# Attention turns put in another order on every engine, and a slot loop written out, in a fused cross-attention and mixture-of-experts kernel

## What is computed

```python
x = x + _L0_xattn_ref(_layernorm(x, axis=-1), ctx_2048, ...)
x = x + _L0_ffn_ref(_layernorm(x, axis=-1), L0_ffn_gate_w, L0_ffn_w1, L0_ffn_w2)
# attention
q = rms_norm(linear(x, q_w, q_b), norm_q_w)
k_img = rms_norm(linear(ctx_img, k_img_w, k_img_b), norm_k_img_w)
v_img = linear(ctx_img, v_img_w, v_img_b)
img_x = attention(q, k_img, v_img)
return linear(out, o_w, o_b)
# experts
topw, sel = jax.lax.top_k(softmax(x @ gate_w.T), 2)
act = jax.nn.silu(g) * u          # g, u = split(x @ w1.T)
out = sum over the two experts of (act @ w2.T) * topw
```

## Time and profile before

| | us |
|---|---|
| median of 3 runs | 558.54 |
| all runs | 558.28, 558.54, 558.55 |
| the profiled execution | 557.55 |
| its span, first to last instruction | 556.0 |

### The profile page before, as it was taken

How to read it: one execution, slowest core, us unless ns; L and a number is a source line. 1 busy time by engine, 2 the same in 40 slices (tenths; PEclk the granted TensorE clock), 3 DMA queues, 4 the chain that set the end, 5 groups by cost and what they waited for, 6 DMA issues and landing times.

```text
span 556.0 us, 15244 instructions
## 1 busy us (share of the span) xinstructions
PE 444.1 (80%) x4192; PEld 397.1 (71%) x4193; DVE 389.4 (70%) x1215; ACT 315.1 (57%) x934; POOL 301.8 (54%) x531
## 2 busy tenths in 40 slices
PE   1779889898989898989898860599999999999100
PEld 1658778777877787778777650499989999999100
DVE  7448888988988898889888855254545454545284
ACT  5357577767776777677767620255555555555100
POOL 6534357777777777777776646044434443444200
PEclk9779899999999999999999985599999999999655
DMA  7131442222322232213221115423434343331499
GB/s 228 53 109 42 128 125 85 75 80 63 89 70 82 62 91 71 82 60 92 65 80 61 50 40 134 134 88 114 127 109 120 102 124 106 116 110 66 164 399 343
DMA packets 49542, 60.30 MB, mean 108 GB/s; under 512 B 7615, under 2 KB 43082, under 8 KB 49482
## 3 DMA queue, kind: packets, MB, share of 16 engines
q1 hardware_dynamic: 38026, 38.00, 23.5%
q0 software_dynamic: 6528, 16.86, 8.8%
q10 hardware_dynamic: 4928, 4.72, 2.5%
HBM read 32.86 MB, written 23.27 MB: 101 GB/s over the span
## 4 chain that ended last, share of the span: by engine, by line
PE 55%; DVE 11%; issue 9%; ACT 9%; POOL 6%; DMA 5%; SPq 3%; POOLq 0%; ACTq 0%; DVEq 0%
PE bank L1109 13%; PE bank L1110 12%; PE bank L1111 12%; PE bank L1320 4%; DMA we_l<-expert_out 3%; DVE late L835 3%; POOL r_qk L415 2%; PE bank L1117 2%; PE bank L1142 2%; PE bank L1219 2%; PE bank L1339 1%; PE bank L1338 1%; ACT square L599 1%; ACT late L554 1%; SPq L382 1%
## 5 line engine op out<-in xcount | busy, mean ns | idle before, releaser
L527 POOL DMA_INDIRECT expert_out<-probs,late x72 | 69.9, 971 | 100.7 <-ACT probs L720 99.6
L457 POOL DMA_INDIRECT sorted_rows<-row,place_i x64 | 66.0, 1031 | 36.3 <-POOL row L451 25.4
L1067 DVE TENSOR_TENSOR xt_l<-bank,xt_h 128x256 fp32r<-128x256 f32 x72 | 30.6, 425 | 54.9 <-ACT xt_h L702 54.8
L564 ACT CAST qp_h<-bank 32x256 f16<-32x256 f32 x128 | 46.4, 363 | 35.7 <-PE bank L1142 33.4
L841 DVE TENSOR_TENSOR qp_l<-bank,qp_h 32x256 f16<-32x256 f32 x128 | 53.3, 416 | 6.0 <-ACT qp_h L564 2.9
L1109 PE MATMUL bank<-we_h,xt_h 128*128 x144 | 53.4, 371 | 0.1
L1074 DVE SCALAR_TENSOR_TENSOR probs<-xn,late,bank 128x176 f32<-128x176 f32 x72 | 28.6, 398 | 33.1 <-ACT xn L708 33.1
L1109 PE MATMUL bank<-we_h,at_h 128*128 x144 | 46.5, 323 | 1.1 <-issue 0.6
L1110 PE MATMUL bank<-we_l,xt_h 128*128 x144 | 47.1, 327 | 0.0
L1111 PE MATMUL bank<-we_h,xt_l 128*128 x144 | 47.0, 326 | 0.0
L708 ACT ACTIVATE xn<-bank 128x176 f32<-128x176 f32 x72 | 22.9, 317 | 38.8 <-PE bank L1111 38.8
(11 more groups left out here) (194 smaller groups left out, 1571.2 us busy)
## 6 DMA issues: line engine op xcount, KB each, us to landing
late<-sorted_rows SPq DMA_DIRECT2D x72, 129.0 KB, 2.1
we_f<-w_exp SPq DMA_DIRECT2D x32, 152.0 KB, 2.5
v_bd<-v_sb SPq DMA_DIRECT2D x128, 34.0 KB, 1.9
ctx_in<-ctx_t SPq DMA_DIRECT2D x32, 128.0 KB, 2.4
we_h<-expert_out SPq DMA_DIRECT2D x8, 512.0 KB, 6.9
we_l<-expert_out SPq DMA_DIRECT2D x8, 512.0 KB, 15.5
x<-x SPq DMA_DIRECT2D x3, 1024.0 KB, 6.0
out<-we_h ACTq DMA_DIRECT2D x8, 256.0 KB, 13.3
```

Source lines behind the costliest of these rows:

```text
L457: pool.indirect_dma_start(sorted_rows, bass.IndirectOffsetOnAxis(ap=place_i[:, t.slot // 2, k, t.par:t.par + 1], axis=0), row[:, k, t.slot ...
L527: pool.indirect_dma_start(expert_out, bass.IndirectOffsetOnAxis(ap=hs[:, r, D:D + 1].bitcast(U32), axis=0), y_sb[:, r % YRING, :], None, b ...
L564: act.copy(q_part(qp_h, t, g), q_bank(g)).then_inc(S["q_h_ready"], 1)
```

## The change

All four computing engines get a new order within each attention turn. `inv_sqrt` on GpSimd is parted: the addition of epsilon is `add_eps`, so that `ln1` becomes `ln1_root` and `ln1_shift`, and `ln2` becomes `ln2_veps` and `ln2_root`, one turn later. `send` loses its first instruction, which becomes `set_ids`. VectorE's `ln2_mean` moves one turn on. `ctx_hi`, `ctx_lo` and the load of the context go one tile further ahead, and `xt_hi`, `k_hi`, `tr_x` and `tr_k` go from the head of a turn to the end of the turn before. The slot loops of all five engines are written out. No computation is added or taken away.

```diff
@@ -341,8 +341,8 @@
         sp.dma_start(sorted_rows[NE * REG:ROWS, :], pad_rows[:, :]).then_inc(pads_sent, 16)
 
         def turn(j, s):
-            if Tile(j, s + 2).live:
-                load_ctx(Tile(j, s + 2))
+            if Tile(j, s + 3).live:
+                load_ctx(Tile(j, s + 3))
             if Tile(j, s + 1).live and (not isinstance(j, int) or j * SKEW + s + 1 >= 2):
                 load_weights(Tile(j, s + 1))
             if Tile(j, s).live:
@@ -407,17 +408,22 @@
             pool.tensor_tensor(we_l[:, cols], we_f[:, t.par, :], we_h[:, cols].bitcast(F32),
                                ALU.subtract).then_inc(S["we_ready"], 1)
 
-        def inv_sqrt(t, out_, tmp, in_, scale, eps, ready, mid, done_):
+        def add_eps(t, out_, in_, scale, eps, ready, done_):
 
             need_alone(pool, pool_passed, ready, t.n + 1)
-            pool.tensor_scalar(tmp, in_, scale, eps, ALU.mult, ALU.add).then_inc(mid, 1)
-            need_alone(pool, pool_passed, mid, t.n + 1)
-            pool.tensor_tensor(out_, tmp, half_neg[:, 0:tmp.shape[1]], ALU.pow).then_inc(done_, 1)
-
-        def ln1(t):
+            pool.tensor_scalar(out_, in_, scale, eps, ALU.mult, ALU.add).then_inc(done_, 1)
+
+        def inv_sqrt(t, out_, in_, ready, done_):
+
+            need_alone(pool, pool_passed, ready, t.n + 1)
+            pool.tensor_tensor(out_, in_, half_neg[:, 0:in_.shape[1]], ALU.pow).then_inc(done_, 1)
+
+        def ln1_root(t):
             need_alone(pool, pool_passed, S["xn_ready"], t.n - 1)
-            inv_sqrt(t, rstd[:, t.slot, :], veps[:, t.slot, :], mean_var[:, t.par, 1:2], 1.0, 1e-5,
-                     S["ln1_mean"], S["ln1_veps"], S["ln1_rstd"])
+            add_eps(t, veps[:, t.slot, :], mean_var[:, t.par, 1:2], 1.0, 1e-5, S["ln1_mean"], S["ln1_veps"])
+            inv_sqrt(t, rstd[:, t.slot, :], veps[:, t.slot, :], S["ln1_veps"], S["ln1_rstd"])
+
+        def ln1_shift(t):
             need_alone(pool, pool_passed, S["ln1_rstd"], t.n + 1)
             pool.tensor_scalar(shift[:, t.par, :], mean_var[:, t.par, 0:1], rstd[:, t.slot, :], -1.0, ALU.mult, ALU.mult
                                ).then_inc(S["ln1_shift"], 1)
...
@@ -460,20 +471,26 @@
                 ).then_inc(row_sent[t.slot], 16)
 
         def turn(j, s):
-            if Tile(j, s + 1).live:
-                ctx_lo(Tile(j, s + 1))
             if Tile(j, s + 2).live:
-                ln1(Tile(j, s + 2))
+                ln1_root(Tile(j, s + 2))
+            if Tile(j, s - 4).live:
+                ln2_root(Tile(j, s - 4))
             if Tile(j, s).live:
                 qk_rms(Tile(j, s))
-            if s % 2 == 0 and Tile(j, s - 6).live:
-                weights(Tile(j, s - 6), Tile(j, s - 5), (s - 6) // 2 % 2)
+            if Tile(j, s - 5).live:
+                set_ids(Tile(j, s - 5))
+            if Tile(j, s).live:
+                weights_lo(Tile(j, s))
             if Tile(j, s - 6).live:
                 send(Tile(j, s - 6))
+            if Tile(j, s + 2).live:
+                ctx_lo(Tile(j, s + 2))
+            if s % 2 == 1 and Tile(j, s - 5).live:
+                weights(Tile(j, s - 5), Tile(j, s - 4), (s - 5) // 2 % 2)
+            if Tile(j, s + 2).live:
+                ln1_shift(Tile(j, s + 2))
             if Tile(j, s - 3).live:
-                ln2(Tile(j, s - 3))
-            if Tile(j, s).live:
-                weights_lo(Tile(j, s))
+                ln2_veps(Tile(j, s - 3))
 
         setup(pool.memset(ident[:, :], 0.0))
         setup(pool.memset(half_neg[:, :], -0.5))
@@ -493,8 +510,9 @@
                                  base=0, pattern=[[-1, P]], channel_multiplier=1))
         setup(pool.affine_select(out=upto[:, :, :], in_=upto[:, :, :], compare_op=ALU.is_ge, fill=0.0,
                                  base=0, pattern=[[1, NE], [-1, NE]], channel_multiplier=0))
-        ln1(Tile(0, 0))
-        ln1(Tile(0, 1))
+        for n in range(2):
+            ln1_root(Tile(0, n))
+            ln1_shift(Tile(0, n))
         ctx_lo(Tile(0, 0))
         for base in (0, -NH):
             after()
@@ -519,6 +537,7 @@
         for q in (qp_h, qp_l):
             pool.memset(q[:, :, :, :, :, :].rearrange("p u b c g l -> p (u b c g l)").bitcast(F32), 0.0
                         ).then_inc(q_cleared, 1)
+        ctx_lo(Tile(0, 1))
         turns_sp(pool, turn)
 
 
@@ -643,14 +662,6 @@
                 t.quads_ok = not static or t.n >= 4
                 t.at = t.n if static else bass.ds(t.n, 1)
                 return t
-            if tile(0).live:
-                xt_hi(tile(0))
-            if tile(1).live:
-                k_hi(tile(1))
-            if tile(-1).live:
-                ln1_norm(tile(-1))
-            if tile(-1).live:
-                ctx_hi(tile(-1))
             if tile(1).live:
                 t = tile(1)
                 t.first = isinstance(j, int) and t.n == 0
@@ -660,18 +671,26 @@
             if tile(0).live:
                 k_square(tile(0))
             if tile(0).live:
+                v_copy(tile(0))
+            if tile(0).live:
                 q_square(tile(0))
             if tile(3).live:
                 att_hi(tile(3))
+            if tile(-1).live:
+                ln1_norm(tile(-1))
+            if tile(-2).live:
+                ctx_hi(tile(-2))
             if tile(0).live:
-                v_copy(tile(0))
-            if tile(0).live:
+                k_scale(tile(0))
                 weights_hi(tile(0))
-                k_scale(tile(0))
+            if tile(2).live:
+                softmax_exp(tile(2))
             if tile(4).live:
                 row_copy(tile(4))
-            if tile(2).live:
-                softmax_exp(tile(2))
+            if tile(0).live:
+                k_hi(tile(0))
+            if tile(-1).live:
+                xt_hi(tile(-1))
             if s % 2 == 1 and tile(5).live:
                 gap_exp(tile(5), tile(4), (s - 5) // 2 % 2)
 
@@ -691,6 +710,8 @@
         act.wait_ge(pool_setup, SETUP_POOL_FIRST)
         act.activation(bias_f, bias_f, ACT.Copy, scale=zero_one[:, 1:2]).then_inc(bias_parts_ready, 1)
         ln1_norm(t)
+        xt_hi(t)
+        ctx_hi(Tile(0, 1))
         split_hi(1)
         turns_sp(act, turn)
         send_pads(act, 1)
...
@@ -957,41 +980,43 @@
                 t.at = t.n if static else bass.ds(t.n, 1)
                 t.sent = t.quad * 32 if t.quads_ok else None
                 return t
-            ahead = tile(-2) if tile(-2).live else None
+            n = j * SKEW + s if isinstance(j, int) else None
+            if tile(1).live:
+                k_lo(tile(1))
             if tile(0).live:
                 xt_lo(tile(0))
-            if isinstance(j, int) and j == s == 0:
+            if n == 0:
                 rest_of_setup()
-            if tile(1).live:
-                k_lo(tile(1))
+                ln1_stats(tile(-2), x_second)
             if tile(2).live:
                 find_max(tile(2))
-            if ahead:
-                n = j * SKEW + s + 2 if isinstance(j, int) else None
-                ln1_stats(ahead, {2: x_second, 8: x_third, 9: x_rest}.get(n))
+            if tile(4).live:
+                ln2_mean(tile(4))
             if tile(2).live:
                 neg_max_hi(tile(2))
+                neg_max_lo(tile(2))
             if tile(3).live:
                 invert_sums(tile(3))
-            if tile(2).live:
-                neg_max_lo(tile(2))
+            if tile(-2).live:
+                ln1_mean(tile(-2))
             if tile(3).live:
                 normalise(tile(3))
-            if ahead:
-                ln1_mean(ahead)
             if tile(1).live:
                 q_lo(tile(1))
+            if tile(3).live:
+                att_lo(tile(3))
             if tile(4).live:
                 ln2_norm(tile(4))
-            if tile(3).live:
-                att_lo(tile(3))
+            if tile(-3).live:
+                ln1_stats(tile(-3), {5: x_third, 13: x_rest}.get(n))
+            if n == 0:
+                fold_gate()
+            if tile(0).live:
+                q_scale(tile(0))
             if s % 2 == 1 and tile(5).live:
                 route(tile(5), tile(4), (s - 5) // 2 % 2)
-            if isinstance(j, int) and j == s == 0:
-                fold_gate()
             if tile(0).live:
                 gate_of_x(tile(0))
-                q_scale(tile(0))
             if tile(3).live:
                 residual(tile(3))
             if s % 2 == 0 and tile(4).live:
@@ -1275,29 +1300,32 @@
 
                 return min(value, NT) if static else value
 
-            if tile(0).live:
-                tr_x(tile(0))
-            if tile(1).live:
-                tr_k(tile(1))
+            if tile(3).live:
+                weigh(tile(3))
             if tile(2).live:
                 t = tile(2)
                 t.first = static and i == 2
                 score_max(t)
-            if tile(3).live:
-                weigh(tile(3))
             if tile(1).live:
                 tr_q(tile(1))
```

(31 more changed lines are left out.)

20 lines of the change are left out of this document (12 added, 8 removed).

## The result

The kernel after took 561.1 us (median of 20 runs, 557.06 to 563.2), the kernel before 558.17 in the same set (20 runs): a ratio of 1.0044, with a 95% interval of 1.0024 to 1.0064. The forecast was 539.0, the range 532.5 to 547. The prediction was wrong: instead of 3.5% faster, the kernel came out 0.4% slower.

A forecast was written before the change was run, and what follows sets the result against it. Attention was taken as bound by GpSimd in heavy turns, by GpSimd and TensorE in light ones. Gains of 12.8 us there and 6.7 in the experts, 19.5 together, took 557.55 to 538.05, median 539.0 us; range 532.5 to 547.

The forecast's parts named there:

- the part on TensorE: Attention stage: TensorE's pieces summed to 8.2 us, `tr_q` finding its keys split; with the late exponential a turn becomes 8.35.
- D: Rival at the sends: behind `weights_lo` GpSimd empties, then prepares, 0.82 atop 0.30; pair 19.5, time 565 us; chance 0.04.
- GpSimd's sum: Attention stage: GpSimd's turn as one loop from `r_qk` to `r_qk`, 9.53 us heavy and 8.34 light.
- the 0.30 chosen: GpSimd: the first send was taken to start 0.30 us after `weights_lo`, its preparing hidden behind that instruction.
- B: Rival at the sends: their preparing isn't hidden, 0.5 more each turn, pair 18.9, time about 553 us; chance 0.10.
- the 0.82: GpSimd's wait in us ahead of the first send in the profile, read as preparing the transfer, ended by no other engine.
- The heavy turn: GpSimd's attention turn with `weights` in it, put at 9.53 us and bound by GpSimd.
- The light turn: GpSimd's attention turn without `weights`, put at 8.34 us, bound by GpSimd and TensorE both; the wait for `q_square` gone.
- TensorE's turn of 8.35: Attention stage: pieces of 8.2 us plus 0.15 for the late exponential; the light half of the 17.88 pair.
- The forecast for the experts: Expert stage: writing out the slots removes the cost of four loop edges and the entry, 6.7 us, the upper bound.
- The 16 pairs of the sum: Attention stage: 16 pairs of turns, each 17.88 instead of 18.70 us, gain 12.8 us; filling and draining left as they are.
- one slow stretch more or less: Clock rival: a stretch of TensorE at half the clock, 6.8 us long, moves the time by up to 2.7 us.

The follow-up runs named there:

- e20: The kernel after, unchanged, run again on another chip: 532.81 us, ratio 0.960.
- e0: The kernel before, unchanged, profiled once more: 556.33 us, a single run.
- e7: The kernel after with GpSimd's two sends moved ahead of `weights_lo`: 565.02 us, ratio 1.012.
- e10: The kernel before with one change, `weigh` ahead of `score_max` on TensorE: 567.4 us, ratio 1.014.
- e13: The kernel after with `score_max` ahead of `weigh` again and GpSimd's sends ahead of `weights_lo`: 564.31 us, ratio 1.012.
- e14: The kernel after with `score_max` ahead of `weigh`; sends ahead of `weights_lo` in turns with `weights`, behind it in turns with `choose`: 535.73 us, ratio 0.960.
- e17: The kernel after, unchanged, run again on another chip beside e18: 561.01 us, ratio 1.005.
- e19: The kernel after, unchanged, run again on one more chip: 559.43 us, ratio 1.001.
- e1: The kernel after with `score_max` put back ahead of `weigh` on TensorE: 545.86 us, ratio 0.977.
- e11: The kernel after with one wait more: `score_max` waits until TensorE's own products of `weigh` are reported: 578.79 us, ratio 1.035.
- e6b: The kernel after with GpSimd's two sends moved behind `ctx_lo`, 0.7 us later: 570.92 us, ratio 1.022.
- e9b: The kernel after with each indirect send replaced by a plain transfer of the same bytes, rows in token order: 537.53 us, ratio 0.964.
- e16: As e14, GpSimd's order by turn, but with `weigh` ahead of `score_max` as in the kernel after: 530.44 us, ratio 0.954.
- e18: e16 unchanged, run again on the same chip as e17: 544.42 us, ratio 0.975.

## Why the prediction was wrong

- **The step that failed** is in the part on TensorE: its pieces were taken at their modelled length and their readers as starting when they end, "so that `tr_q` finds its keys split". That the order of `weigh` and `score_max` could matter was not weighed, and none of the rivals had it. In the execution measured, reports were held until 0.6 us behind the second send, so those of `score_max` and `tr_q` came at 3.1 us, and the long turn became 10.53 instead of 9.34 (e20), the short one 8.97 instead of 8.36. From the seventh `tr_q` to the last are 243.3 us, where 12.5 pairs at 17.88 make 223.5: **19.8** of the 22.1 us that were missed. The experts' part missed 0.8 in this pair of traces. The other 1.5 are a balance that I did not split: the turns up to the seventh `tr_q` came out shorter (54.5 instead of 59.1), the way from the last `tr_q` to the first slot longer (40.5 instead of 38.8).
- **Could the rows have told?** No. The trace of before is of the kind without a hold (report 1.2 beside the same sends), and a second trace of the same kernel (e0) had it, at hardly any cost. D, the slower rival, hit the pair, 19.5, by the wrong mechanism; that was luck.
- **GpSimd's sum was right in size, and in part by luck.** The first send starts 0.17 after `weights_lo`, even less than the 0.30 chosen, and B and D fell with it. But the reason given was wrong: the 0.82 were read as the preparing of a transfer that no engine ends, while the row names GpSimd's own copy, and e7 has 0.17 with no long instruction ahead. In e20 `r_qk` starts at 160.32, 168.66 and 178.03. The heavy turn is 9.37 with no wait but the one at `weights_lo`; of the 0.16 below the forecast 0.13 are the send's gap. The light turn is 8.34, to the digit, but by luck: it has a wait of 0.35 for `q_square` in it that the prediction held to be gone, so there GpSimd is not what bounds it. TensorE's turn of 8.35 came out at 8.36, the pair at 17.71. `weights_lo` waits 0.8 for `weights_hi`, as said.
- **`k_lo`.** In e20 `tr_q` waits for it 2.8 us in all; in the first trace of after 11.7. The sentence quoted above holds where the reports are prompt, and less where they are held.
- **Experts.** First to last slot: 156.71 before, 149.92 in e20, so 6.8 instead of 6.7. In the first trace of after a slot of 3.23 us stands in the middle, and 5.9 are left:

```profile
477.53 0.38 PE L1353 MATMUL bank<-ident,late 128*128 128x128 f32 x2
479.65 0.38 PE L1353 MATMUL bank<-ident,late 128*128 128x128 f32 x2
482.88 0.44 PE L1353 MATMUL bank<-ident,late 128*128 128x128 f32 x2 [0.21 <-issue]
485.04 0.38 PE L1353 MATMUL bank<-ident,late 128*128 128x128 f32 x2
```

  A slot of 2.8 to 3.2 us at this very place is in every trace from the six chips with held reports, and in neither of the other two. It does not come of writing the slots out, for e0 and e10, whose slots are a loop, have it too (3.21 and 3.17). So the 5.9 compare a trace of one kind with one of the other: within the kind with held reports it is 158.25 (e0) against 150.85, 7.4 less. The forecast for the experts was right; the cause of the slow slot wasn't tried.
- **The filling.** The 16 pairs of the sum count the filling turns with 0.8 a pair like all others. From the first to the seventh `tr_q`, three pairs, before took 59.1 in its first trace and 54.1 in e0, e20 52.5: 6.6 or 1.6 gained, where the sum has 2.4. The 12.5 pairs behind them gained 12.0 instead of 10.0. Against the first trace of before that is 6.2 more than the sum has, 4.2 of it because the filling was slow in that one trace; some 1 us was lost elsewhere, and the profiled e20, 532.86, is 5.2 below the 538.05 of the forecast. It lies at the lower end of the range.
- **The clock.** The prediction allowed for one slow stretch more or less, up to 2.7 us. That was enough for after and e20, but in e13 a change of order brought ten of them and some 14.5 us, and in e7 eleven.

## What to carry to other kernels

An engine's piece in a timeline ends where the profiler puts it; when its product is available is read from who starts behind it, and in a pipeline of engines that is what counts. Before a reordering is costed, look at these readers beside every indirect transfer of GpSimd, and take traces of the same kernel on more than one chip: one with no visible delay is no evidence that there is none, above all where nobody waits for it. Keep what is awaited away from the time just around such sends, and keep GpSimd's computing steps away from VectorE's short chains; e14 does both and gained 4.0% on a chip with held reports, where the plain reordering lost 0.1 to 0.5% on two others of that kind (e17, e19). Compare the granted clock of the stretches too: a wait of TensorE that recurs in every turn can cost a good part of its length once more by the clock.

## What was new about the hardware

- On six of eight chips, reports of TensorE's products that fell beside GpSimd's indirect sends came 0.5 to 0.8 us after a send's end (after: 175.82 to 176.43; e1: 169.34 to 169.99; e11: 181.44 to 181.98; e6b is the exception, up to 1.0 after its first send), 1.9 late in after and up to 2.2 in e10. VectorE's was not held: in the same turn `tr_q` starts 0.14 after `k_lo` ends (175.66 to 175.80). Plain transfers by GpSimd held nothing (e9b). The same program took 2.6% (e16, e18) or 5% (e20 against e17 and e19) more where they were held.
- An indirect send starts 0.17 after the instruction ahead of it when all that it waits for is long done, be that instruction 0.83 long (after) or 0.19 (e7); where the copy ahead of it writes what it waits for, it starts 0.82 after it.
- Short instructions of VectorE (2 and 4 elements per lane) lasted until GpSimd's instruction beside them had ended: on average 0.95 to 1.02 us instead of 0.14 for the one, 0.56 to 0.60 instead of 0.17 for the other (e7, e13).
- Behind a wait of TensorE of 1.93 us its granted clock was 0.50 for 3.4 us, and the turn took 1.45 us longer (e13).
